# Attention with two-expert routing on one core: the order of the convolutions, of the maxima, of the high parts and of the scatters

## The chip, the cores and the metric

The kernel runs on one core of one Trainium2 chip. The metric is the device time of one launch in microseconds (us). Three runs of the kernel before took 3302.37, 3303.25 and 3305.23 us; the median is 3303.25 us.

## What is computed

The input x is 8 images of 128 channels and 32x32 positions. Each image is normalised over its channels and gets a position table; then

```python
q = conv2d(inp, wq)                 # 1x1
k = conv2d(inp, wk, 1, 1)           # 3x3
v = conv2d(inp, wv, 1, 1)           # 3x3
q = q * cos + rotate_every_two(q) * sin
k = k * cos + rotate_every_two(k) * sin
attn = softmax(q @ k.T * SCALE)     # 8 heads, 1024 x 1024 each
attn = einsum('bhij,hg->bgij', attn, mix)
out  = conv2d(attn @ v, wo) + bo    # then a * sigmoid(g), added to x
```

A second layer follows: each of the 8192 tokens is normalised, sent to its best two of eight experts (128 to 512 to 128, with gelu), and the weighted sum is added. Everything is fp32.

## The kernel before, in words

**Precision.** A fp32 number is split into a high part (fp32r) and a low part (the rest). A product takes three matmuls: high weight with low data, low with high, high with high (`split3`, L662).

**Batches and units.** The attention handles one image (a batch) after the other. A batch has a first stretch ("conv stage" here) and then 16 units of 512 queries: unit u is head u//2, half u%2. The keys of a unit are cut in eight chunks of 128 (`kc`). Batches 1 to 6 are one hardware loop; batches 0 and 7 are written out. In batch b, the units also carry the routing of image b-1 (the first layer's result), and late units prepare the input of image b+1.

**Conv stage.** `conv(b, g)` (L705) makes 12 groups of 128 channels x 512 positions: g 0 to 3 are q, 4 and 5 the lower half of k's channels (heads 0 to 3), 6 and 7 the upper half (heads 4 to 7), 8 to 11 are v. k and v have nine taps of three matmuls each. The four PSUM banks of `conv_bank` (L85) are used in turn by g % 4. Groups 0 to 7 are rotated: VectorE multiplies by cosine and shuffles neighbours (L1311), GpSimd multiplies by sine and adds (L541), ScalarE rounds the high part (`rot_hi`, L1048), VectorE subtracts it (`rot_lo`, L1320). The four scratch halves `rot_a`, `rot_s` (L180) lie in the tile E32. SyncE's queue copies q and k of each head from `src` into the stacks `kst`, `qst` (`stacks`, L377), six DMAs a head; for head 0 it waits for the sixth `rot_lo`. v goes through `v_copy` (L1061), transposes on TensorE (`v_transpose`, L756), `v_hi` (L1067) and `v_lo` (L1345). Between these lie the output projection, gate and routing rows of image b-1, and the maxima and first scores of units 0 and 1.

**Maxima.** Softmax needs a shift for each query. For each of a unit's four blocks of 128 queries TensorE computes scores into a two-bank tile, MA or MB (`max_scores`, L765), VectorE takes the maximum (`take_max`, L1352), ScalarE sums the exponentials (`sums`, L1078), and VectorE works out the shift in 14 tiny instructions (`shifts`, L1357, parts 0, 1 and 2). `max_row` (L776) turns the shifts into two rows of `qst` by way of MA and `row_copy` (L1073). This runs two to three units ahead.

**A unit.** At step kc TensorE runs the six value matmuls of the chunk (`values`, L791, into the two PV banks), one `scores` matmul (L784) six chunks ahead into ST[kc % 2], and, for a coming unit, `max_scores` at steps 1, 3, 5 and 7 (L806 to L851). ScalarE turns each score tile into E32 (`exps`, L1084), GpSimd rounds it into the high part Eh (`cast`, L524), VectorE subtracts into El (`exp_lo`, L1394), and `values` uses both. At the end ScalarE empties the two PV banks, scaled by mix (`evict`, L1090, at step 7), and GpSimd adds them to `acc` from unit 3 on (`add`, L534, at steps 0 and 3). The order on each engine is written by hand, in the functions `unit` and `batch` of GpSimd (L567, L587), TensorE (L806, L853), ScalarE (L1118, L1147) and VectorE (L1519, L1553). An engine runs its instructions in that order; a wait holds all that follow it.

The values of a unit start with a wait for the `evict` of the unit before (L797):

```python
            def values(b, u, kc):
                n = b * UNITS + u
                wait(pe, *low(n, kc))
                for c in range(2):
                    ...
                    if kc == 0:
                        wait(pe, s_ev, 2 * n - 1 + c)
```

and on ScalarE a `sums` stands ahead of that `evict` (L1135, at step 6, where L1121 puts the evictions at step 7).

**Routing.** Units 0 to 5 of a batch carry VectorE's small routing steps (`route`, L1413), units 3 and 4 ScalarE's `row_norm` (L1109). In unit 6 GpSimd copies the rows (`row_pair`, L553), and in units 6 to 9 it issues 16 indirect DMAs, `scatter` (L561), four a unit, at odd steps. The buffer they leave is the one into which SyncE then loads image b+1 (L416 to L421), for `prepare` (L679) from unit 12 on.

Of the kernel before, what the change touches and what calls it, by code (L numbers as in the profile page):

```python
# [6 lines left out]
B, C, IMG = 8, 128, 32  # L7
# [40 lines left out]
def build(nc, x, wq, wk, wv, mix, wo, bo, wr, br, ln_g, ln_b, w1, b1, w2, b2,  # L48
# [18 lines left out]
    with ctx:  # L67
# [17 lines left out]
        def conv_bank(g):  # L85

            return [ST[0][:, :], ST[1][:, :], MB[:, 0:NB], MB[:, NB:2 * NB]][g % 4]

# [91 lines left out]
        rot_a = [E32[:, 2 * i, :] for i in range(2)]  # L180
        rot_s = [E32[:, 2 * i + 1, :] for i in range(2)]
# [172 lines left out]
        def _(sp):  # L354
# [145 lines left out]
        def _(pool):  # L500
# [23 lines left out]
            def cast(b, u, kc):  # L524


                if isinstance(b, int):
                    pool.wait_ge(s_ex, KC * (b * UNITS + u) + kc + 1)
                else:
                    pool.wait_ge(s_ex, ready[kc % 2])  # L530
                    pool.reg_add(ready[1 - kc % 2], ready[kc % 2], 1)
# [9 lines left out]
            def rotate(b, g):  # L541

                a, s = rot_a[g % 2], rot_s[g % 2]
# [23 lines left out]
            def unit(b, u, prev):  # L567
                for kc in range(KC):
                    if prev is not None and u == 6 and kc == 0:
                        paired(prev)  # L570
                    if prev is not None and u == 6 and kc == 1:
                        placed(prev)
# [23 lines left out]
            pool.reg_mov(ready[0], KC * UNITS + 1)  # L596
# [61 lines left out]
        def _(pe):  # L658
# [46 lines left out]
            def conv(b, g, taps=None):  # L705
# [4 lines left out]
                if g >= 4 and (taps is None or taps[0] == 0):  # L710
                    wait(pe, s_rf, b * 8 + g - 3)
                o = conv_bank(g).rearrange("p (y x) -> p y x", x=IMG)
# [93 lines left out]
            def unit(b, u, prev, more):  # L806

                n = b * UNITS + u
                for kc in range(KC):
# [35 lines left out]
                    if kc == KC - 1:  # L845
                        if u < UNITS - 3:
                            if prev is not None and u == 4:
                                pe.wait_ge(s_pr, prev + 2)
                            if more and u == UNITS - 4:
                                pe.wait_ge(s_cent, (b + 1) * 2 + 2)  # L850
# [937 lines left out]
```

## Time and profile before

| | us |
|---|---|
| median of three runs | 3303.25 |
| the profiled execution | 3300.94 |
| its span, first to last instruction | 3299.2 |
| TensorE busy | 2969.2 |
| VectorE busy | 2327.6 |
| ScalarE busy | 1730.2 |
| GpSimd busy | 1530.1 |

The attention (batches 0 to 7) fills the span up to about 2900 us, the experts the rest. In batch 3, which is used as the example, the conv stage starts at 1096.8 us, unit 1 at 1208.1 us, and the next batch's conv stage at about 1459 us. A matmul's duration in the rows is its own latency: in an undisturbed stream the starts lie 0.23 us apart though each lasts 0.39 us. "g" or "idle before" is the time in which an engine had nothing running before an instruction, and the name behind it what ended that.

### The profile page before, as it was taken

The page shows a single profiled execution, that of the slowest core. Times are in us where ns is not written, and L with a number is a line of the kernel's source. Part 1 is how long each engine was busy: PE and PEld are TensorE (multiplying, and loading weights), DVE is VectorE, ACT ScalarE, POOL GpSimd, SP SyncE. Part 2 cuts the span into 40 slices and gives each one's busy share as a digit, 9 for nine tenths or more (in the row PEclk, how much of TensorE's full clock was granted, in tenths as well). Part 3 has the DMA queues.
Part 4 walks back from the last instruction along what each step waited for, and adds up shares of the span by engine and source line. Part 5 has one row for each costly group of instructions (what it writes and reads, how often), then busy time and mean ns, then how long its engine had stood idle before and what let it go on. Part 6 is the DMA issues. An engine that isn't in the chain of part 4 may idle for free.

```text
span 3299.2 us, 45985 instructions
## 1 busy us (share of the span) xinstructions
PE 2969.2 (90%) x13024; PEld 2350.6 (71%) x13024; DVE 2327.6 (71%) x4556; ACT 1730.2 (52%) x2996; POOL 1530.1 (46%) x1729
## 2 busy tenths in 40 slices
PE   7999989898989899898989899898989898949997
PEld 5777777676767777676767677676767677737776
DVE  4688658874888568864978478865887488845664
ACT  2566346542666256643655266634655366626671
POOL 3244515642364425552464335551565236525783
PEclk9999999999999999998999999999999999969998
DMA  4254010101011001101110101101010101216665
GB/s 144 81 210 156 17 26 22 35 15 32 20 31 28 20 24 34 35 2 33 30 33 17 34 20 27 32 18 26 22 33 15 32 20 41 63 59 218 237 227 210
DMA packets 71320, 196.22 MB, mean 59 GB/s; under 512 B 16134, under 2 KB 16720, under 8 KB 71028
## 3 DMA queue, kind: packets, MB, share of 16 engines
q1 hardware_dynamic: 61940, 175.88, 17.4%
q0 software_dynamic: 9088, 16.94, 1.6%
q8 instruction: 123, 2.02, 0.3%
q14 instruction: 169, 1.38, 0.1%
HBM read 39.91 MB, written 63.34 MB: 31 GB/s over the span
## 4 chain that ended last, share of the span: by engine, by line
PE 54%; issue 14%; DVE 10%; POOL 9%; ACT 8%; DMA 3%; SPq 2%; ACTq 0%; POOLq 0%; DVEq 0%
PE PVT L660 34%; PE ST L660 9%; PE MB L660 6%; PE MA L660 5%; DVE nmax L1355 3%; POOL Eh L532 3%; POOL E L545 2%; POOL E L547 2%; ACT tmp L1025 2%; ACT E L1025 2%; POOL rows L563 1%; DMA wt<-wall 1%; DVE El L1397 1%; ACT MA L1025 1%; POOL acc L539 1%
## 5 line engine op out<-in xcount | busy, mean ns | idle before, releaser
L532 POOL CAST Eh<-E 128x512 fp32r<-128x512 f32 x1024 | 684.8, 671 | 1335.1 <-ACT E L1025 1327.0
L1397 DVE TENSOR_TENSOR El<-E,Eh 128x512 fp32r<-128x512 f32 x1024 | 925.6, 905 | 368.1 <-POOL Eh L532 365.1
L660 PE MATMUL PVT<-El,vh 128*128 128x512 f32 x2048 | 849.1, 415 | 158.6 <-ACT tmp L1025 111.0
L1025 ACT ACTIVATE E<-ST 128x512 f32<-128x512 f32 x1024 | 610.4, 598 | 671.9 <-PE ST L660 644.5
L660 PE MATMUL PVT<-Eh,vl 128*128 128x512 f32 x2048 | 819.1, 400 | 0.0
L660 PE MATMUL PVT<-Eh,vh 128*128 128x512 f32 x2048 | 817.2, 399 | 0.0
L660 PEld LDWEIGHTS PVT<-El,vh 128*128 128x128 f32 x2048 | 395.8, 193 | 299.9 <-ACT tmp L1025 125.4
L1025 ACT ACTIVATE MA<-MA,nmax 128x1024 f32<-128x1024 f32 x288 | 313.0, 1087 | 277.7 <-DVE nmax L1355 222.0
L660 PEld LDWEIGHTS PVT<-Eh,vh 128*128 128x128 f32 x2048 | 394.5, 193 | 88.0
L660 PEld LDWEIGHTS PVT<-Eh,vl 128*128 128x128 f32 x2048 | 397.3, 194 | 78.2 <-issue 3.4
L1355 DVE TENSOR_REDUCE nmax<-MA 128x1 f32<-128x1024 f32 x288 | 350.7, 1218 | 96.4 <-PE MA L660 95.6
L660 PE MATMUL ST<-qst,kst 98*128 98x512 f32 x1024 | 412.2, 404 | 0.0
L539 POOL TENSOR_TENSOR acc<-acc,tmp 128x512 f32<-128x512 f32 x224 | 288.3, 1288 | 40.3 <-ACT tmp L1025 40.3
L1355 DVE TENSOR_REDUCE nmax<-MB 128x1 f32<-128x1024 f32 x224 | 273.0, 1219 | 0.3 <-PE MB L660 0.3
L1025 ACT ACTIVATE MB<-MB,nmax 128x1024 f32<-128x1024 f32 x224 | 239.2, 1068 | 17.5 <-DVE nmax L1355 17.4
L660 PE MATMUL MA<-kst,qst 96*128 96x512 f32 x576 | 186.5, 405 | 53.8 <-DMA qst<-src 27.9
L660 PEld LDWEIGHTS ST<-qst,kst 98*128 98x128 f32 x1024 | 196.7, 192 | 44.2 <-ACT E L1025 1.7
L628 POOL DMA_INDIRECT yrows<-xr,idx x156 | 190.9, 1224 | 75.0 <-issue 41.8
L545 POOL TENSOR_TENSOR E<-E,sin_sb 128x512 f32<-128x512 f32 x64 | 90.1, 1408 | 200.4 <-DVE E L1318 200.4
L1025 ACT ACTIVATE src<-E 128x512 fp32r<-128x512 f32 x64 | 40.4, 631 | 268.8 <-POOL E L547 268.8
L1025 ACT ACTIVATE tmp<-PVT,mix_col 128x512 f32<-128x512 f32 x224 | 143.8, 686 | 53.8 <-PE PVT L660 53.7
L1686 DVE TENSOR_TENSOR hl<-h,hh 128x1024 fp32r<-128x1024 f32 x78 | 95.7, 1226 | 103.2 <-ACT hh L1025 85.8
(273 smaller groups left out, 4330.0 us busy)
## 6 DMA issues: line engine op xcount, KB each, us to landing
rows<-xr SPq DMA_DIRECT2D x68, 520.0 KB, 5.6
kst<-src SPq DMA_DIRECT2D x192, 128.0 KB
qst<-src SPq DMA_DIRECT2D x192, 128.0 KB
wt<-wall SPq DMA_DIRECT2D x39, 514.0 KB
wt<-wall SPq DMA_DIRECT2D x39, 512.5 KB
xrow<-rows SPq DMA_DIRECT2D x39, 260.0 KB
wall<-yrows SPq DMA_DIRECT2D x32, 256.0 KB, 4.8
xr<-in_x_dram SPq DMA_DIRECT2D x8, 512.0 KB, 3.5
```

The lines of the kernel that those rows point to most:

```text
L532: nc.gpsimd.tensor_copy(Eh[:, kc, :], E32[:, kc % 4, :]).then_inc(s_eh, 1)
L539: nc.gpsimd.tensor_tensor(acc[:, c, cols], acc[:, c, cols], tmp[:, c, :], ALU.add).then_inc(s_acc, 1)
L545: nc.gpsimd.tensor_tensor(s, s, sin_sb[:, g % 2 * NB:(g % 2 + 1) * NB], ALU.mult).then_inc(s_rot, 1)
L547: nc.gpsimd.tensor_tensor(a, a, s, ALU.add).then_inc(s_rr, 1)
L563: nc.gpsimd.indirect_dma_start(out=rows_d[:, :], out_offset=bass.IndirectOffsetOnAxis(ap=slot[:, i:i + 1], axis=0), in_=xr[c][:, g, :], in ...
L628: nc.gpsimd.indirect_dma_start(out=yrows_d[:, :], out_offset=bass.IndirectOffsetOnAxis(ap=idx[j % XR][:, i:i + 1], axis=0), in_=yrow[j % Y ...
L660: return nc.tensor.matmul(o, w, m, start=start, stop=stop)
L1025: return nc.scalar.activation(o, i, func, **kw)
L1355: nc.vector.tensor_reduce(nmax[:, par, i:i + 1], M[:, :], AX, ALU.max, negate=True).then_inc(s_red, 1)
L1397: tt(El[:, kc, :], E32[:, kc % 4, :], f(Eh[:, kc, :]), ALU.subtract).then_inc(s_lo, 1)
L1686: tt(low, exact, f(high), ALU.subtract).then_inc(t_hl, 1)
```

## The change

1. **Order of the convolutions.** The upper half of k (groups 6 and 7) is convolved after v (groups 8 to 11). `turn` gives the place of each group in that order, from which its bank and its semaphore counts follow. Groups 6 and 7 are rotated in the tiles `tmp` and `eg` instead of E32. The stacks of head 4 wait for the last two `rot_lo`. The order of everything else in the conv stage is rewritten around it, and VectorE rotates group 4 ahead of the first gate.
2. **Maxima at chunks 1, 3, 4 and 6.** TensorE's `max_scores` of steps 5 and 7 move to steps 4 and 6, VectorE's `take_max` with them, ScalarE's `sums` of step 6 to step 5, VectorE's `shifts` parts 1 and 2 from step 6 to step 7.
3. **High parts.** For chunks 1 and 7 ScalarE writes Eh itself, with a second exponential of the same score tile, and GpSimd's cast is gone.
4. **Scatters.** Three a unit at steps 5, 6 and 7 of units 6 to 11 (3, 3, 3, 3, 3, 1) instead of four a unit in units 6 to 9. GpSimd's `add` moves from steps 0 and 3 to steps 1 and 3, `placed` from step 1 to step 4 of unit 6.

```diff
+        turn = [0, 1, 2, 3, 4, 5, 10, 11, 6, 7, 8, 9]
...
-        rot_a = [E32[:, 2 * i, :] for i in range(2)]
-        rot_s = [E32[:, 2 * i + 1, :] for i in range(2)]
+        rot_a = [E32[:, 2 * (g % 2), :] for g in range(6)] + [tmp[:, 0, :], eg[:, 0, :]]
+        rot_s = [E32[:, 2 * (g % 2) + 1, :] for g in range(6)] + [tmp[:, 1, :], eg[:, 1, :]]
...
-                if h == 0:
-                    sp.wait_ge(s_rlo, b * 8 + 6)
+                if h % 4 == 0:
+                    wait(sp, s_rlo, b * 8 + 6 + h // 2)
...
             def cast(b, u, kc):
+                if kc in (1, 7):
+                    return
...
-                    if kc in (0, 3) and u >= 3:
-                        add(b, u - 1, kc // 3)
+                    if kc in (1, 3) and u >= 3:
+                        add(b, u - 1, kc // 2)
...
-                    if prev is not None and 6 <= u < 10 and kc % 2 == 1:
-                        scatter(prev, 4 * u - 24 + kc // 2)
+                    if prev is not None and 6 <= u < 12 and kc in (5, 6, 7) and 3 * u - 23 + kc < 2 * KC:
+                        scatter(prev, 3 * u - 23 + kc)
...
             def batch(b, prev=None):
-                for g in range(8):
+                for g in range(6):
                     rotate(b, g)
-                for kc in range(AHEAD):
+                cast(b, 0, 0)
+                rotate(b, 6)
+                cast(b, 0, 2)
+                rotate(b, 7)
+                for kc in range(3, AHEAD):
                     cast(b, 0, kc)
```

TensorE, in `unit` and then in `batch`:

```diff
+                    if kc == 4 and u < UNITS - 3:
+                        max_scores(b, u + 3, 0, MA, 4 * n + 11)
                     if kc == 5:
-                        if u < UNITS - 3:
-                            max_scores(b, u + 3, 0, MA, 4 * n + 11)
...
-                    if kc == KC - 1:
-                        if u < UNITS - 3:
...
-                            max_scores(b, u + 3, 1, MB, 4 * n + 12)
+                    if kc == 6 and u < UNITS - 3:
...
+                        max_scores(b, u + 3, 1, MB, 4 * n + 12)
...
-                conv(b, 6)
-                conv(b, 7, range(0, 5))
+                conv(b, 8)
+                conv(b, 9)
                 if prev is not None:
                     pe.wait_ge(s_gate, prev * 2 + 2)
                 max_scores(b, 0, 0, MA, 4 * n)
-                conv(b, 7, range(5, TAPS))
                 if prev is not None:
                     route_rows(prev)
+                conv(b, 10, range(0, 5))
                 max_scores(b, 0, 1, MA, 4 * n + 1)
...
+                conv(b, 10, range(5, TAPS))
                 if prev is not None:
                     route_logits(prev)
...
+                max_scores(b, 0, 2, MA, 4 * n + 2)
+                conv(b, 11, range(0, 5))
                 if prev is not None:
                     pe.wait_ge(s_lg, prev + 1)
                 v_transpose(b, 0)
+                max_scores(b, 0, 3, MA, 4 * n + 3)
+                conv(b, 11, range(5, TAPS))
+                max_scores(b, 1, 0, MA, 4 * n + 4)
+                v_transpose(b, 1)
+                conv(b, 6, range(0, 5))
                 max_row(b, 0, 4 * n + 5)
-                conv(b, 10, range(0, 5))
+                conv(b, 6, range(5, TAPS))
                 pe.wait_ge(s_mrow, n + 1)
                 max_scores(b, 1, 1, MA, 4 * n + 5)
-                pe.wait_ge(s_vt, b * 4 + 2)
+                pe.wait_ge(s_vt, b * 4 + 4)
                 scores(b, 0, 0)
+                v_transpose(b, 2)
+                conv(b, 7, range(0, 3))
                 scores(b, 0, 1)
...
                 max_scores(b, 1, 2, MA, 4 * n + 6)
+                conv(b, 7, range(3, 6))
+                v_transpose(b, 3)
                 scores(b, 0, 2)
...
                 max_scores(b, 1, 3, MA, 4 * n + 7)
+                conv(b, 7, range(6, TAPS))
                 scores(b, 0, 3)
...
                 scores(b, 0, 4)
                 max_scores(b, 2, 0, MA, 4 * n + 8)
...
                 scores(b, 0, 5)
+                pe.wait_ge(s_rf, b * 8 + 8)
                 max_scores(b, 2, 1, MB, 4 * n + 8)
```

ScalarE, in `exps`, `unit` and `batch`, and VectorE, in `exp_lo`, `unit` and `batch`:

```diff
+                if kc in (1, 7):
+                    copy(Eh[:, kc, :], ST[1][:, :], ACT.Exp)
                 copy(E32[:, kc % 4, :], ST[kc % 2][:, :], ACT.Exp).then_inc(s_ex, 1)
...
-                    if kc == 6 and u < UNITS - 3:
+                    if kc == 5 and u < UNITS - 3:
                         sums(b, u + 3, 0, MA)
...
-                rot_hi(b, 6)
-                sums(b, 0, 0, MA)
-                rot_hi(b, 7)
+                v_copy(b, 0)
+                v_copy(b, 1)
                 if prev is not None:
                     row_transposed(prev)
+                sums(b, 0, 0, MA)
                 sums(b, 0, 1, MA)
+                v_copy(b, 2)
                 sums(b, 0, 2, MA)
...
                 sums(b, 1, 2, MA)
+                rot_hi(b, 6)
+                v_hi(b, 3)
                 exps(b, 0, 2)
                 sums(b, 1, 3, MA)
                 exps(b, 0, 3)
...
+                rot_hi(b, 7)
                 exps(b, 0, 4)
                 sums(b, 2, 0, MA)
...
-                dve.wait_ge(s_eh, KC * n + kc + 1)
+                if kc in (1, 7):
+                    dve.wait_ge(s_ex, KC * n + kc + 1)
+                else:
+                    wait(dve, s_eh, 6 * n + max(kc, 1))
...
-                    if u < UNITS - 2 and kc == 6:
+                    if u < UNITS - 2 and kc == 7:
                         shifts(b, u + 2, 1)
...
-                    if u < UNITS - 2 and kc == 6:
+                    if u < UNITS - 2 and kc == 7:
                         shifts(b, u + 2, 2)
...
-                    if u < UNITS - 3 and kc in (5, 7):
-                        take_max(b, u + 3, kc // 2 - 2, MA if kc == 5 else MB)
+                    if u < UNITS - 3 and kc in (4, 6):
+                        take_max(b, u + 3, kc // 2 - 2, MA if kc == 4 else MB)
...
+                rotate(b, 4)
+                rot_lo(b, 4)
                 if prev is not None:
                     gate(prev, 0)
-                rotate(b, 4)
-                rot_lo(b, 4)
```

## Rows read from the trace of the kernel before

**Rows 1.** The page: busy us, share of the span and instructions of each engine.

```profile
PE 2969.2 (90%) x13024; PEld 2350.6 (71%) x13024; DVE 2327.6 (71%) x4556; ACT 1730.2 (52%) x2996; POOL 1530.1 (46%) x1729
```

**Rows 2.** Stretches of batch 3: from:to, length, busy us per engine, granted clock, DMA.

```profile
1096.80:1191.30 94.50, 80.15 (x326) 61.73 (x324) 45.05 (x88) 28.66 (x48) 28.52 (x24) 0.91 0.11 29
1208.14:1396.08 187.94, 172.60 (x758) 136.88 (x758) 160.36 (x331) 121.05 (x219) 102.01 (x123) 0.98 0.14 35
1208.14:1223.80 15.66, 15.31 (x69) 12.17 (x69) 13.44 (x37) 10.62 (x20) 5.16 (x8) 1.00 0.23 51
1255.76:1272.35 16.59, 16.29 (x77) 13.12 (x77) 14.79 (x33) 12.22 (x25) 8.24 (x10) 1.00 0.00 1
1325.32:1344.30 18.98, 15.29 (x68) 12.16 (x68) 15.68 (x28) 10.87 (x20) 12.55 (x14) 1.00 0.05 16
1396.08:1413.88 17.80, 17.34 (x72) 12.78 (x73) 15.22 (x29) 10.57 (x20) 7.59 (x10) 1.00 0.00 1
```

**Rows 3.** Waits of TensorE over the span: us in total, times, longest us.

```profile
PE PVT L660 <- ACT tmp L1025: 111.0, 85, 3.7
PE PVT L660 <- DVE vl L1349: 37.5, 15, 3.0
...
PE MA L660 <- DMA qst<-src: 27.9, 7, 6.1
PE MA L660 <- ACT MA L1025: 24.4, 8, 3.8
```

**Rows 4.** Timeline of TensorE and ScalarE where unit 1 ends: start, us, instruction.

```profile
1222.82 0.62 PE L660 MATMUL MB<-kst,qst 96*128 96x512 f32 x2
1223.80 0.50 PE L660 MATMUL PVT<-El,vh 128*128 128x512 f32 x1 [0.35 <-ACT acc L1025]
...
1221.96 1.09 ACT L1025 ACTIVATE MA<-MA,nmax 128x1024 f32<-128x1024 f32 x1
...
1223.06 1.26 ACT L1025 ACTIVATE acc<-PVT,mix_col 128x512 f32<-128x512 f32 x2
```

**Rows 5.** Timeline of unit 8, a unit with scatters: GpSimd, VectorE, ScalarE, TensorE.

```profile
1329.27 1.30 POOL L539 TENSOR_TENSOR acc<-acc,tmp 128x512 f32<-128x512 f32 x1
...
1329.34 2.32 DVE L1397 TENSOR_TENSOR El<-E,Eh 128x512 fp32r<-128x512 f32 x1 [1.52 <-POOL Eh L532]
...
1339.32 1.25 POOL L563 DMA_INDIRECT rows<-xr,slot  x1 [0.17 <-ACT E L1025]
...
1341.14 1.21 DVE L1355 TENSOR_REDUCE nmax<-MA 128x1 f32<-128x1024 f32 x1
...
1342.47 1.09 ACT L1025 ACTIVATE MA<-MA,nmax 128x1024 f32<-128x1024 f32 x1 [3.29 <-DVE lman L1376]
...
1343.35 0.69 DVE L1397 TENSOR_TENSOR El<-E,Eh 128x512 fp32r<-128x512 f32 x1
...
1344.30 0.50 PE L660 MATMUL PVT<-El,vh 128*128 128x512 f32 x1 [3.70 <-ACT tmp L1025]
```

**Rows 6.** Groups over the span: count | busy us, mean ns | idle before.

```profile
L532 POOL CAST Eh<-E 128x512 fp32r<-128x512 f32 x1024 | 684.8, 671 | 1335.1 <-ACT E L1025 1327.0 <-issue 3.9 <-POOL xr L554 1.2
L1025 ACT ACTIVATE E<-ST 128x512 f32<-128x512 f32 x1024 | 610.4, 598 | 671.9 <-PE ST L660 644.5 <-DVE El L1397 26.7 <-issue 0.2
...
```

**Rows 7.** Timeline, batch 3 conv stage: TensorE stall, two conv matmuls, VectorE's sixth `rot_lo`.

```profile
1136.33 0.73 PE L660 MATMUL MA<-kst,qst 96*128 96x512 f32 x2 [3.62 <-DMA qst<-src]
...
1145.60 0.40 PE L660 MATMUL ST<-xl,wch 128*128 128x512 f32 x1
1145.84 0.40 PE L660 MATMUL ST<-xh,wcl 128*128 128x512 f32 x1
...
1129.81 0.69 DVE L1324 TENSOR_TENSOR src<-E,src 128x512 fp32r<-128x512 f32 x1 [3.43 <-ACT src L1025]
```

**Rows 8.** Next image: DMA issue (page; last: us to landing), its first matmul.

```profile
xr<-in_x_dram SPq DMA_DIRECT2D x8, 512.0 KB, 3.5
...
1400.54 1.12 PE L660 MATMUL MB<-xr,mean_w 128*128 128x512 f32 x2 [0.17 <-ACT MB L1025]
```

More of the change, by code:

```diff
@@ L529, in cast @@
                 else:
-                    pool.wait_ge(s_ex, ready[kc % 2])
-                    pool.reg_add(ready[1 - kc % 2], ready[kc % 2], 1)
+                    pool.wait_ge(s_ex, ready[i])
+                    pool.reg_add(ready[1 - i], ready[i], 2 if kc in (0, 6) else 1)
                 nc.gpsimd.tensor_copy(Eh[:, kc, :], E32[:, kc % 4, :]).then_inc(s_eh, 1)
@@ L570, in unit @@
                         paired(prev)
-                    if prev is not None and u == 6 and kc == 1:
+                    if prev is not None and u == 6 and kc == 4:
                         placed(prev)
@@ L595, in _ @@
             batch(0)
-            pool.reg_mov(ready[0], KC * UNITS + 1)
+            pool.reg_mov(ready[1], KC * UNITS + 1)
             with pool.Fori(1, B - 1) as b:
@@ L709, in conv @@
                     pe.wait_ge(s_xin, b + 1)
-                if g >= 4 and (taps is None or taps[0] == 0):
-                    wait(pe, s_rf, b * 8 + g - 3)
-                o = conv_bank(g).rearrange("p (y x) -> p y x", x=IMG)
+                if taps is None or taps[0] == 0:
+                    if 4 <= turn[g] < 10:
+                        wait(pe, s_rf, b * 8 + turn[g] - 3)
+                    elif turn[g] >= 10:
+                        wait(pe, s_vt, b * 4 + turn[g] - 9)
+                o = conv_bank(turn[g]).rearrange("p (y x) -> p y x", x=IMG)
                 every = [4] if kind == 0 else list(range(TAPS))
@@ L844, in unit @@
                             prefix(prev)
-                    if kc == KC - 1:
-                        if u < UNITS - 3:
[L847 to L850, printed above, removed]
-                            max_scores(b, u + 3, 1, MB, 4 * n + 12)
+                    if kc == 6 and u < UNITS - 3:
+                        if prev is not None and u == 4:
+                            pe.wait_ge(s_pr, prev + 2)
+                        if more and u == UNITS - 4:
+                            pe.wait_ge(s_cent, (b + 1) * 2 + 2)
+                        max_scores(b, u + 3, 1, MB, 4 * n + 12)
             def batch(b, prev=None, more=True):
@@ L1050, in rot_hi @@
                 act.wait_ge(s_rr, b * 8 + g + 1)
-                copy(src[:, 2 * kind, c, hf * NB:(hf + 1) * NB].bitcast(f32r), rot_a[g % 2]).then_inc(s_rhi, 1)
+                copy(src[:, 2 * kind, c, hf * NB:(hf + 1) * NB].bitcast(f32r), rot_a[g]).then_inc(s_rhi, 1)
             def out_hi(n, hf):
@@ L1061, in v_copy @@
             def v_copy(b, g):
[L1062 removed]
+                act.wait_ge(s_cv, b * 12 + 6 + g + 1)
                 if g >= 2:
                     wait(act, s_vT, b * 4 + g - 1)
[L1065 removed]
+                copy(vt[g % 2][:, :], conv_bank(turn[8 + g])).then_inc(s_vt, 1)
             def v_hi(b, g):
@@ L1182, in batch @@
                 exps(b, 0, 3)
-                v_copy(b, 3)
-                v_hi(b, 2)
+                rot_hi(b, 7)
                 exps(b, 0, 4)
                 sums(b, 2, 0, MA)
-                v_hi(b, 3)
                 exps(b, 0, 5)
@@ L1585, in batch @@
                     shifts(b, 0, part)
+                v_lo(b, 0)
                 take_max(b, 1, 0, MA)
-                v_lo(b, 0)
+                v_lo(b, 1)
+                rotate(b, 6)
                 take_max(b, 1, 1, MA)
                 exp_lo(b, 0, 0)
-                v_lo(b, 1)
+                v_lo(b, 2)
+                exp_lo(b, 0, 1)
                 take_max(b, 1, 2, MA)
-                exp_lo(b, 0, 1)
+                rot_lo(b, 6)
+                v_lo(b, 3)
                 exp_lo(b, 0, 2)
                 take_max(b, 1, 3, MA)
-                exp_lo(b, 0, 3)
+                rotate(b, 7)
                 for part in range(3):
                     shifts(b, 1, part)
-                v_lo(b, 2)
+                exp_lo(b, 0, 3)
                 take_max(b, 2, 0, MA)
                 exp_lo(b, 0, 4)
-                v_lo(b, 3)
+                rot_lo(b, 7)
                 take_max(b, 2, 1, MB)
```

45 lines of the change are left out of this document (13 added, 32 removed).

## Prediction

> **What bounds the kernel now.** I read the page first: TensorE is busy for 2969.2 of 3299.2 us, every other engine far less [rows 1]. So only two things can shorten the kernel: TensorE's pauses, and the stretches at half clock. Next the stretches of batch 3. A plain unit lasts 15.66 us with 15.31 busy, so it has almost no pause; unit 8, with scatters, lasts 18.98 us with the same 15.29 busy; units 1 to 11 together last 187.94 us; the conv stage has 80.15 busy in 94.50 us at a mean granted clock of 0.91, that is partly at 1.2 instead of 2.4 GHz [rows 2]. The table of waits then names the pauses: 111.0 us in 85 waits for an eviction of the PV banks, at the start of a unit, 37.5 us for `v_lo`, 27.9 us for head 0's stacks, 24.4 us for a `sums` [rows 3].
>
> The timeline shows why the eviction is late. When unit 1 ends, ScalarE starts the `sums` of unit 4's first block at 1221.96, which holds it till 1223.06; only then come the two evictions (1.26 us), though the first bank was complete about 1 us earlier. TensorE issued its last two matmuls at 1222.82; at 0.23 us each it could have gone on at 1223.28 and starts at 1223.80, 0.52 us late [rows 4]. In a unit with scatters the same queue is longer: the maximum on VectorE starts at 1341.14, the `sums` only at 1342.47 after 3.29 us of idleness, and TensorE starts 3.70 us late at 1344.30 [rows 5]. The maximum was ready long before, but VectorE's order puts it behind an El subtraction and six shift instructions, and that subtraction waits for a cast which stands behind an add and a scatter on GpSimd.
>
> **The change, part by part.**
>
> *Maxima at steps 4 and 6.* Nothing is added. The first block's `sums` leaves step 6, next to the eviction, for step 5. Counting with T as the start of chunk 7's values: the first bank is done at T + 0.9, ScalarE is then free (its chunk-4 exponential ends about T + 0.35), so the first eviction ends at T + 1.6 and TensorE can go on at T + 1.7, against T + 1.6 at which it is ready. Of the 0.52 us some 0.1 stays: 0.4 us a plain unit, 15.66 to 15.25. The reuse of MA and MB costs nothing: `sums` of the same tile ends 1.8 us before the earlier `max_scores` in a plain unit. What is late next is the shift. The last maximum is issued at T - 0.46 and starts on VectorE at T + 0.2; a maximum and part 1 of the shifts behind it take 2.2 us (1341.14 to 1343.35 [rows 5]), then come an El subtraction and part 2 with some 0.9 together: T + 3.3, and TensorE reaches `max_row` at T + 3.4. It just fits, with no cover left. In units from 3 on an add holds VectorE once more: a subtraction that should take 0.69 takes 2.32 us beside a 1.30 us add [rows 5]. I put such units at 15.5.
>
> *Two high parts on ScalarE.* GpSimd loses 256 casts of 0.67 us, ScalarE gains 256 exponentials of 0.60 us (153 us) against 671.9 us of idleness ahead of its exponentials [rows 6]. They fall in steps 1 and 3, which have no `sums`. ScalarE is then at 12 of 15.3 us in a plain unit, nearly full in units 3 and 4 with `row_norm`. The bounds: nothing, or 0.60 on the path in each of 128 units (77 us). I take nothing, since a score tile is used again only two steps, 3.5 us, later.
> The trace shows the subtraction stretched beside the add, as said [rows 5]. The Trainium skill (SBUF — State Buffer, "SBUF: two separate sides") says that a VectorE instruction with two SBUF inputs and a GpSimd instruction that reads SBUF exclude each other for their whole length, and that ScalarE never waits. By that rule the two missing casts free VectorE too, by at most 2 x 0.67 us a unit; my sum has nothing for it.
>
> *Scatters.* 16 indirect DMAs as before, 1.25 us each [rows 5], three in a row at steps 5 to 7, each behind a cast. With six casts (4.0), two adds (2.6) and three scatters (3.8) GpSimd has 10.4 us a unit, where it had 12.55 in unit 8 [rows 2]. Chunks 4 to 6 get their high part up to 1.3 us later, chunk 6 is needed last of all, and no eviction stands behind them any more. So I put units 7 to 10 at 15.7, unit 6 with its row copy at 16.0, unit 11 at 15.5. Unit 4 has 0.9 us more matmuls (it is 16.59 with 16.29 busy [rows 2]): 16.4. With two plain units at 15.25 and units 3, 5, 11 at 15.5 the sum is 30.5 + 46.5 + 16.4 + 16.0 + 62.8 = 172.2 against 187.94: **-15.7 us a batch**. Unit 12 starts 0.4 us sooner (17.80 to 17.4 [rows 2]).
> The last scatter moves from unit 9 to unit 11, step 5, and SyncE's queue holds the load of the next image behind it. That scatter starts about 13.1 us into the unit, lands some 2.5 us later (an estimate from its 1.25), the load takes 3.5 us and its issue 0.5: 19.6 us. The image's first matmul comes 4.46 us into unit 12 (1400.54 - 1396.08 [rows 2, 8]), so at 19.8. Nothing to one microsecond a batch; I take nothing.
>
> *Conv stage.* The matmuls are the same. Head 0's stacks still wait for the sixth `rot_lo` (1129.81), because the rotation of group 4 is now ahead of the gate and that of group 5 behind it: same time. But TensorE now has two whole groups of v (54 matmuls, starting every 0.24 us [rows 7], 13.0 us) before it needs them, where it had 14 taps (42 matmuls, 10.1 us): the 3.62 us stall [rows 7] falls to 0.7. The two `v_lo` stalls at the first values, 37.5 us in 15 waits [rows 3] and so 2.5 us each, vanish, since v is ready before. New waits stand in for them: `v_copy` of the third group waits for the first v transpose and holds a `sums` (2.0 us); VectorE's queue with rotation 6, and ScalarE's with `rot_hi` 6 and 7, hold the maxima of unit 1 (0.5 + 3.7 + 2.3) and chunk 4's exponential and `sums` inside unit 0 (1.2 + 2.4). Laid out by hand, unit 0's second half of values (1191.3 now [rows 2]) starts at 1183.6, and 3.6 us are lost again behind it: -4, with a microsecond for the clock **-5 us a batch**. The bounds are far apart: -10 (the new waits hidden) to +4 (each twice as long).
>
> **Sum.** Six looped batches: -(15.7 + 0.4 + 5) = -21.1, together -127. Batch 7, which prepares no image, -19. Batch 0 has no scatters: 13 units of -0.4 and -4 in the conv stage, -9. That is -155. I keep 12 us back, 1.5 a batch, for waits of the new order that a hand schedule overlooks: **-143**. The profiled execution, 3300.94 us (span 3299.2), goes to 3158; it lies 2.3 us below the median of 3303.25, which goes to **3160 us**.
>
> **Rivals.**
> *A, the shift becomes the bound.* VectorE's chain to `max_row` has no slack, and VectorE is busy for 15.7 us in unit 8 [rows 2]. For it: the 2.32 us subtraction. Against: the adds fall at other steps. If `max_row` waits 0.5 to 0.6 us in each of 12 units a batch, 52 us go: about 3210.
> *B, the scatters in a row cost as much as before.* A cast behind each scatter is late by 1.25 us, three times. Against: nothing that ends a unit waits for them. If units 6 to 10 keep 1.6 us each, 56 us go in seven batches: 3216. The Trainium skill (SBUF — State Buffer, the box on SWDGE) says that a VectorE operation on the shared port keeps GpSimd from writing descriptors; by that rule it is three scatters in a row that would suffer.
> *C, everything moved is hidden.* The conv stage gives 10 us a batch and VectorE's freed time takes the rest: 3303 - 185 = 3118.
> *D, slower.* One mechanism: `max_row` held by the shifts, by so much that the unit is longer than now. Units 1 to 11 average 17.1 us now [rows 2]. With -40 us from the conv stages the change loses once they last over some 17.6 us, which means part 2 ending at T + 5.6, 2.3 us later than I count; the last maximum and the subtraction would each have to meet an add. At 17.9 us in every unit it is +0.8 x 11 x 7 and, for batch 0's 13 plain units, +2.2 each: 3303 + 62 + 29 - 40 = 3354.
> *E, nothing.* Should the pause at a unit's start move whole to another step, the time stays 3300.
>
> **How the numbers follow.** Forecast 0.68; A 0.14; B 0.05; C 0.08; D 0.03; E 0.02. The forecast's own range is 3130 to 3190. The middles of A, B and C lie inside 3115 to 3225, but each has a spread of some 30 us either way (the conv stage's bounds alone are -5 and +9 us in eight batches, -40 and +72), so this range holds about 8 in 10. What a measurement can tell from no change is about 0.2%, 6.6 us. All but D and E are faster by more: faster 0.95, same 0.02, slower 0.03.
>
> **What would show it.** Right: waits for the eviction fall from 111 us to under 30, plain units last 15.2 to 15.4 and units 7 to 10 under 16.2, El waits on GpSimd less, the `v_lo` stall is gone and the stack stall is below 1.5 us. New small waits before `max_row`'s MA matmuls and for `sums` late in the conv stage. Wrong: a wait for VectorE's `mc` of over 0.3 us in each unit (A, D), units 7 to 10 above 17 (B), a wait for the image's DMA in unit 12, or a longer conv stage.

## The result, and the profile after

The changed kernel takes **3246.37 us** (median of 4 runs, 3242.84 to 3250.75), the kernel before 3303.01 beside it: ratio 0.9828, 95% interval 0.9811 to 0.9845. That is 56.6 us less where 143 were forecast, and outside both ranges (3130 to 3190, and the wider 3115 to 3225). Its profiled execution took 3247.52 us.

The page of the changed kernel, busy time by engine, against [rows 1]:

```profile
PE 2948.0 (91%) x13024; PEld 2298.3 (71%) x13024; DVE 2381.6 (73%) x4556; ACT 1877.4 (58%) x3252; POOL 1362.3 (42%) x1473
```

TensorE is busy for 21.2 us less with the same 13,024 matmuls. It ran longer at the full clock: the mean granted clock of the profiled span is 0.965, and was 0.949. ScalarE has the 256 new exponentials, GpSimd lost 256 casts. Next TensorE's waits, as in [rows 3]:

```profile
PE MA L670 <- ACT MA L1039: 79.1, 43, 3.8
PE MA L670 <- DVE mc L1408: 78.0, 109, 2.6
...
PE MA L670 <- DMA qst<-src: 11.3, 10, 3.1
```

The 111.0 us for evictions and the 37.5 us for `v_lo` are gone, the wait for the stacks fell from 27.9 to 11.3. In their place stand 78.0 us for `mc`, the input of `max_row`, in nearly every unit, and three times the wait for a `sums` in bank MA (24.4 before). The stretches of batch 3: units 1 to 11, the plain unit 1, unit 4, unit 6 (the row copy), unit 8, unit 12:

```profile
1195.63:1376.85 181.22, 171.28 (x758) 132.67 (x757) 162.72 (x330) 133.83 (x241) 87.16 (x101) 1.00 0.14 33
1195.63:1211.62 15.99, 15.47 (x69) 11.93 (x68) 13.72 (x37) 11.77 (x22) 4.13 (x6) 1.00 0.22 49
1243.53:1261.61 18.08, 16.54 (x79) 12.94 (x78) 16.03 (x34) 13.61 (x27) 6.56 (x8) 1.00 0.00 0
1277.51:1295.53 18.02, 15.39 (x70) 12.02 (x69) 16.25 (x27) 11.88 (x22) 9.38 (x12) 1.00 0.02 5
1311.97:1327.86 15.89, 15.38 (x69) 12.02 (x69) 13.93 (x25) 11.89 (x22) 9.67 (x12) 1.00 0.04 14
1376.85:1394.99 18.14, 17.63 (x73) 12.55 (x72) 15.78 (x29) 11.98 (x22) 6.76 (x8) 1.00 0.10 31
```

Against [rows 2]: units 1 to 11 last 181.22 us instead of 187.94, and 172.2 was the forecast. Unit 8 went from 18.98 to 15.89, as forecast. The plain unit, forecast at 15.25, went *up* from 15.66 to 15.99, unit 4 from 16.59 to 18.08, unit 12, forecast at 17.4, from 17.80 to 18.14. `max_row` waits in each of the eleven: 0.52, 0.52, 0.55, 1.54, 0.34, 2.63, 0.88, 0.51, 1.01, 0.51, 0.94 us, together 9.95 of idle time, a little more than the 9.0 that are missing.

How the wait comes about is seen where unit 1 gives way to unit 2 (the chunk 7 of unit 1 starts at T = 1209.98). Timeline of VectorE, then GpSimd's cast and TensorE:

```profile
1210.18 1.23 DVE L1371 TENSOR_REDUCE nmax<-MB 128x1 f32<-128x1024 f32 x1
1211.33 0.15 DVE L1392 SCALAR_TENSOR_TENSOR lman<-lman,lfit 128x4 f32<-128x4 f32 x1
...
1212.31 0.16 DVE L1402 TENSOR_TENSOR shft<-shft,lfit 128x4 f32<-128x4 f32 x1
1212.40 0.18 DVE L1460 SCALAR_TENSOR_TENSOR ny<-nt,ny 128x16 f32<-128x16 f32 x1
1212.52 0.69 DVE L1416 TENSOR_TENSOR El<-E,Eh 128x512 fp32r<-128x512 f32 x1
1213.13 0.58 DVE L1406 CAST mc<-shft 128x4 fp32r<-128x4 f32 x1
1213.74 0.16 DVE L1408 TENSOR_TENSOR mc<-shft,mc 128x4 fp32r<-128x4 f32 x1
...
1212.89 0.80 POOL L538 CAST Eh<-E 128x512 fp32r<-128x512 f32 x1 [1.81 <-ACT E L1039]
...
1214.04 0.40 PE L670 MATMUL MA<-identr,mc 128*2 128x128 f32 x4 [0.52 <-DVE mc L1408]
```

The maximum starts at T + 0.20, as worked out ahead, and the subtraction at T + 2.54, 0.1 later. But the small cast into `mc`, 128x4, takes 0.58 us where it takes 0.17 with nothing beside it: it ends as GpSimd's cast of a high part does (1212.89 + 0.80 = 1213.69). So `mc` is ready at T + 3.92 instead of T + 3.3. TensorE's last matmul before it started at 1213.12, so it could have gone on at 1213.36 or so, T + 3.4 as forecast, and goes on at T + 4.06: 0.7 us late. The 0.52 in the row is less because it counts from the end of that matmul, whose own latency runs on.

A wait can cost more than its length. The 2.63 us of unit 6 are the same in batches 3 and 4, but the unit lasts 18.02 us in one and 19.6 in the other. The stretch of unit 6 in batch 4, to be set beside the fourth line above:

```profile
1630.31:1649.92 19.61, 16.98 (x69) 13.16 (x69) 16.25 (x27) 11.97 (x22) 9.38 (x12) 0.91 0.01 5
```

The mean granted clock is 0.91 there and 1.00 in batch 3: after the pause TensorE ran for a while at the lower of its two levels (1.2 instead of 2.4 GHz).

### The profile page after: what moved, and what is told of

Same layout as the page of the kernel before. It is cut to its first block and busy times, and to the rows that moved or that the text cites. A ratio compares the mean times of both kernels' runs of the same rounds, so it can differ in the third digit from the quotient of the medians.

```text
span 3245.8 us, 45775 instructions
## 1 busy us (share of the span) xinstructions
PE 2948.0 (91%) x13024; PEld 2298.3 (71%) x13024; DVE 2381.6 (73%) x4556; ACT 1877.4 (58%) x3252; POOL 1362.3 (42%) x1473
## 5 line engine op out<-in xcount | busy, mean ns | idle before, releaser
L538 POOL CAST Eh<-E 128x512 fp32r<-128x512 f32 x768 | 536.9, 700 | 1499.9 <-ACT E L1039 1499.0
L1416 DVE TENSOR_TENSOR El<-E,Eh 128x512 fp32r<-128x512 f32 x1024 | 950.9, 931 | 225.9 <-POOL Eh L538 222.6
L670 PE MATMUL PVT<-El,vh 128*128 128x512 f32 x2048 | 836.3, 408 | 0.0
L670 PE MATMUL PVT<-Eh,vl 128*128 128x512 f32 x2048 | 809.7, 395 | 0.0
L670 PE MATMUL PVT<-Eh,vh 128*128 128x512 f32 x2048 | 808.6, 395 | 0.0
L545 POOL TENSOR_TENSOR acc<-acc,tmp 128x512 f32<-128x512 f32 x224 | 295.2, 1321 | 44.9 <-ACT tmp L1039 44.9
L670 PE MATMUL MA<-kst,qst 96*128 96x512 f32 x576 | 195.1, 421 | 60.0 <-ACT MA L1039 48.2
L670 PEld LDWEIGHTS ST<-qst,kst 98*128 98x128 f32 x1024 | 195.9, 191 | 58.0 <-ACT E L1039 15.4
L1039 ACT ACTIVATE tmp<-PVT,mix_col 128x512 f32<-128x512 f32 x224 | 153.7, 688 | 98.5 <-PE PVT L670 98.2
L670 PEld LDWEIGHTS MA<-kst,qst 96*128 96x128 f32 x576 | 106.1, 197 | 110.7 <-ACT MA L1039 58.0
L1039 ACT ACTIVATE Eh<-ST 128x512 fp32r<-128x512 f32 x256 | 153.1, 598 | 34.3 <-PE ST L670 34.2
```

The source lines that it names most:

```text
L538: nc.gpsimd.tensor_copy(Eh[:, kc, :], E32[:, kc % 4, :]).then_inc(s_eh, 1)
L545: nc.gpsimd.tensor_tensor(acc[:, c, cols], acc[:, c, cols], tmp[:, c, :], ALU.add).then_inc(s_acc, 1)
L670: return nc.tensor.matmul(o, w, m, start=start, stop=stop)
L1039: return nc.scalar.activation(o, i, func, **kw)
L1416: tt(El[:, kc, :], E32[:, kc % 4, :], f(Eh[:, kc, :]), ALU.subtract).then_inc(s_lo, 1)
```

## The experiments

The change has four parts here: 1 the order of the convolution, 2 the maxima with the shifts' parts 1 and 2 from step 6 to step 7, 3 the high parts, 4 the scatters and adds. Ratios are to the kernel before, measured beside each.

**e1, the shifts back at step 6.** On VectorE only, all four parts kept otherwise:

```diff
-                    if u < UNITS - 2 and kc == 7:
+                    if u < UNITS - 2 and kc == 6:
                         shifts(b, u + 2, 1)
...
-                    if u < UNITS - 2 and kc == 7:
+                    if u < UNITS - 2 and kc == 6:
                         shifts(b, u + 2, 2)
```

> The changed kernel with one part undone: VectorE makes parts 1 and 2 of the shifts at step 6 again, ahead of the last maximum, not at step 7. Theory V: the gain that is missing went into TensorE's wait for the shifts (mc) at max_row, 78.0 us in 109 waits, because parts 1 and 2 stand behind the last maximum on VectorE. Then this wait falls below 15 us, no other wait at the unit's start takes its place, plain units last 15.2 to 15.4 us instead of 15.8 to 16.0, and the time is 3150 to 3185 us. Rival P: VectorE is held by GpSimd's casts and adds wherever the shifts stand (they met casts at step 7); then max_row waits half as long as now and the time is 3195 to 3225. Rival N: the eviction wait returns or ScalarE's two extra exponentials set the pace; time 3235 to 3255.

**3183.77 us** (3181.66 to 3185.22), ratio 0.9651 [0.9630, 0.9672]: 62.6 us below the change. Its waits of TensorE, then its stretches (units 1 to 11, unit 1, unit 4):

```profile
PE MA L670 <- ACT MA L1039: 79.8, 46, 3.6
...
PE MA L670 <- DVE mc L1408: 8.7, 21, 0.6
```

```profile
1170.90:1345.31 174.41, 170.72 (x759) 133.24 (x758) 165.88 (x326) 134.00 (x241) 88.73 (x101) 1.00 0.14 34
1170.90:1186.18 15.28, 15.28 (x69) 12.01 (x68) 13.73 (x38) 11.75 (x22) 4.10 (x6) 1.00 0.23 51
1216.95:1234.28 17.33, 16.85 (x77) 12.93 (x77) 17.02 (x37) 13.46 (x27) 6.32 (x9) 1.00 0.00 0
```

The plain unit has no pause left: 15.28 long, 15.28 busy. The `mc` waits fell by 69.3 us, and the time by nearly that. The place of eight small instructions a unit (parts 1 and 2) cost 62.6 of the 119 us that the kernel gives with them at step 6.

**e2, part 2 alone** on the kernel before (shifts at step 7, as in the change).

> The kernel before with part 2 of the change alone (maxima at steps 4 and 6, sums at step 5, shifts parts 1 and 2 at step 7); casts, scatters and convolutions as before. Theory V: the eviction waits (111 us) go, and a wait for mc at max_row comes in every unit, somewhat longer than in the changed kernel since GpSimd has all casts: 90 to 130 us. Time 3260 to 3295. Rival: the maxima alone are the whole gain, 3240 to 3255, and the other parts give nothing.

3305.92 us, ratio 1.0014 [1.0, 1.0027]: nothing gained, where I had expected 3260 to 3295. The size of the `mc` waits was as expected; that they would eat the whole gain was not.

```profile
PE MA L660 <- DVE mc L1391: 97.2, 108, 4.0
PE PVT L660 <- DVE vl L1348: 37.1, 15, 3.0
...
PE PVT L660 <- ACT tmp L1024: 6.0, 7, 0.9
```

The wait for evictions went from 111.0 to 6.0 us, and 97.2 us for `mc` came in its place: one wait swapped for another.

**e7, part 2 alone with the shifts at step 6.**

> The kernel before with the order of the maxima of the change on all engines, but the shifts left at step 6, where they were; no other part of the change. With the shifts at step 7 the same edit measured 3305.92 us, nothing gained. Theory V (only the place of the shifts gave the gain away): TensorE's waits for the eviction fall from 111 us below 40 us and no mc waits of the size of the 97 us come in their place; 3215 to 3245 us. Rival (the gain needs the high parts or the scatters of the change too, or VectorE has no time left in a unit): mc or eviction waits stay above 80 us together, 3270 us or more.

3228.56 us, ratio 0.9794 [0.9775, 0.9814]: `mc` waits 31.3 us in 26, eviction waits 8.2. Against e2 the place of the shifts alone is worth 0.022, that is 73 us of 3300. Left are the units with scatters: units 6 to 9 of batch 3 last 17.40, 16.27, 16.60 and 18.88 us.

**e3, part 1 alone.**

> The kernel before with part 1 of the change alone (upper half of k convolved last, with the new order of the conv stage on every engine). The comparison of the two traces puts the conv stage, from the last eviction of a batch to the first of the next, at 111 to 113 us before and 108.3 to 109.5 after; so theory: 3 us a batch, 3275 to 3285 us. Rival: the conv stage gives the whole gain of the change (7 us a batch, 3245 to 3255), or in the surroundings of the old units nothing at all (3300 to 3306).

3288.55 us (3275.53 to 3294.82), ratio 0.9964 [0.9948, 0.9980]. The `v_lo` waits go, the waits for a `sums` grow to 83.2 us, and the evictions keep their 112.4: some 12 us in all, a little less than the 18 to 28 expected.

**e5, part 4 undone in the change** (adds at steps 0 and 3, scatters at the odd steps of units 6 to 9).

> The changed kernel with part 4 undone: four scatters a unit at odd steps in units 6 to 9, adds at steps 0 and 3, the row copy's placing at step 1. Theory V says that GpSimd's load matters only through the casts and adds that hold VectorE's shifts; units 7 to 9, now 16.44, 15.89 and 16.6, get longer by 0.5 to 1.5 us, unit 4 (18.1) and unit 6 (18.0 to 19.6), whose adds and row copy stand at step 1 behind a held shift, shorter: 3240 to 3265 us. Rival S: the new scatter places carry a large part of the gain, 3275 to 3295.

3254.35 us, ratio 0.9871 [0.9845, 0.9897] against 0.9828: 8 us slower by the medians, 14 by the ratios, whose intervals just touch, with `mc` waits of 82.0. The time is in V's range, its units are not: unit 4 stays at 18.09 us, and unit 6 or 7 of a looped batch lasts up to 20.5.

**e8, parts 1 and 2 of the shifts together, still at step 7:**

```diff
                     if u < UNITS - 2 and kc == 7:
                         shifts(b, u + 2, 1)
+                        shifts(b, u + 2, 2)
...
-                    if u < UNITS - 2 and kc == 7:
-                        shifts(b, u + 2, 2)
```

> The changed kernel, parts 1 and 2 of the shifts still at step 7, but part 2 directly behind part 1, ahead of the routing operation and the El subtraction. This takes 0.7 to 1.3 us out of the way of mc in each unit and nothing else. Theory V1 (mc is 0.5 us late because of what stands between the parts and the GpSimd cast that it meets there): mc is ready at T+2.9 instead of T+3.9, mc waits fall from 78 us below 20 us, 3185 to 3205 us. Rival V2 (step 7 is late whatever stands between, since part 1 only begins at T+1.3 behind the maximum): mc waits stay above 50 us, above 3225 us.

3223.32 us, ratio 0.9766 [0.9748, 0.9784], `mc` waits 36.0 us in 31: below V2's bounds, above V1's. V1 holds in the first units: 15.40, 15.15 and 15.62 us in batch 3, as with step 6, so what stood between the parts and the cast met there is what made them late. V1 missed that at step 7 the chain now meets GpSimd in a unit with scatters. Batches 1, 2, 6 and 7 have a unit 9 of 20.0 to 21.6 us. VectorE, GpSimd and TensorE in that of batch 2, then the stretch of this unit:

```profile
967.48 0.66 DVE L1402 TENSOR_TENSOR shft<-shft,lfit 128x4 f32<-128x4 f32 x1
968.17 1.87 DVE L1406 CAST mc<-shft 128x4 fp32r<-128x4 f32 x1
...
967.18 0.98 POOL L569 DMA_INDIRECT rows<-xr,slot  x1 [0.17 <-issue]
968.17 0.62 POOL L538 CAST Eh<-E 128x512 fp32r<-128x512 f32 x1
968.75 1.26 POOL L545 TENSOR_TENSOR acc<-acc,tmp 128x512 f32<-128x512 f32 x1
...
970.37 0.37 PE L670 MATMUL MA<-identr,mc 128*2 128x128 f32 x2 [3.70 <-DVE mc L1408]
...
964.79:986.32 21.53, 17.83 (x70) 13.85 (x69) 16.83 (x28) 11.98 (x22) 10.18 (x13) 0.84 0.20 47
```

A cast of four columns takes 1.87 us, as long as GpSimd's cast and add beside it (968.17 to 970.01), and TensorE stands for 3.70 us. The unit loses more than that, since the clock falls to its lower level behind the pause (0.84 over the unit). The rows before the change had already shown a subtraction held by two instructions of GpSimd in a row: the 2.32 us of [rows 5] are not the add alone (it ends at 1330.57), but also the cast behind it, which the subtraction outlasts by 0.55 us.

```profile
1330.50 0.61 POOL L532 CAST Eh<-E 128x512 fp32r<-128x512 f32 x1
```

**e10, the cast tested by itself:** the changed kernel, part 2 by reductions.

```diff
-                    nc.vector.tensor_copy(mc[:, par, :, 0], z).then_inc(s_ch, 1)
+                    one = z.rearrange("p (a o) -> p a o", o=1)
+                    nc.vector.tensor_reduce(mc[:, par, :, 0], one, AX, ALU.max).then_inc(s_ch, 1)
...
-                    tt(mc[:, par, :, 1], z, f(mc[:, par, :, 0]), ALU.subtract).then_inc(s_ch, 1)
+                    nc.vector.tensor_reduce(mc[:, par, :, 1], one, AX, ALU.max, negate=True).then_inc(s_ch, 1)
```

> The changed kernel with the two small instructions of part 2 of the shifts, the cast of z (128x4) and the subtraction z - mc, replaced by two reductions over an axis of length one, at the same place in VectorE's order and with the same waits. Left out: the low part of the row mc (the second column gets the negated z instead), so the output is another one. Theory L (VectorE's cast and its subtraction are held by the GpSimd cast that runs beside them, 0.58 us in a plain unit where 0.17 is usual; an instruction with one SBUF input and no fast mode is not held): the reductions take 0.2 us each even beside a GpSimd cast, mc is ready 0.4 us sooner, mc waits fall from 78 us to 35 to 50 us, 3205 to 3225 us. Rival (the cast is late for a reason of its own, or everything on VectorE waits beside GpSimd): the first reduction has a mean above 0.4 us like the cast (474 ns), mc waits stay within 10 us of 78, 3240 us or more.

The groups of the changed kernel (two lines) and of this one (two lines): count | busy us, mean ns.

```profile
L1406 DVE CAST mc<-shft 128x4 fp32r<-128x4 f32 x128 | 60.7, 474 | 0.7
L1408 DVE TENSOR_TENSOR mc<-shft,mc 128x4 fp32r<-128x4 f32 x128 | 27.2, 213 | 4.4
```

```profile
L1409 DVE TENSOR_REDUCE mc<-shft 128x4 fp32r<-128x4 f32 x128 | 20.2, 158 | 4.4
L1407 DVE TENSOR_REDUCE mc<-shft 128x4 fp32r<-128x4 f32 x128 | 19.2, 150 | 0.7
```

And the place that was shown above, VectorE, GpSimd, TensorE:

```profile
1211.81 0.15 DVE L1407 TENSOR_REDUCE mc<-shft 128x4 fp32r<-128x4 f32 x1
1211.99 0.16 DVE L1409 TENSOR_REDUCE mc<-shft 128x4 fp32r<-128x4 f32 x1
...
1211.55 0.82 POOL L538 CAST Eh<-E 128x512 fp32r<-128x512 f32 x1 [1.81 <-ACT E L1039]
...
1212.28 0.34 PE L670 MATMUL MA<-identr,mc 128*2 128x128 f32 x3
```

Both run at once, inside GpSimd's cast, and TensorE no longer waits. Over the whole trace, 190 of these reductions have a cast of GpSimd beside them and the longest takes 0.16 us; of the casts into `mc` in the changed kernel 97 have one, with a median of 0.58, and the 16 with nothing beside them have 0.17. So theory L holds for the instructions. For the time it is less clear: `mc` waits 47.9 us and a plain unit lasts 15.4 to 15.6, but that is the fastest run (3214.57); the runs go up to 3243.01, the median is 3233.48 us, 8 above the range, and the ratio, 0.9809 [0.9791, 0.9826], overlaps that of the change. Batch 4 of the profiled run has a unit 9 of 21.31 us where the others have 16.5 to 16.7: there the El subtraction ahead of the reductions is held for 2.49 us (1659.83), and the reductions take 0.14 and 0.16 us behind it. Whether this makes the runs differ by 28 us was not tried.

**Parts 3 and 4.** e4 is the change without part 3; e6 is e1 without part 3, e11 e1 without part 4, e12 e1 without both.

> The changed kernel with all eight high parts cast by GpSimd again, the shifts still at step 7. Beside shifts at step 6 the two casts cost nothing (3182.42 against 3183.77 us). Theory P (where VectorE's chain to mc is the bound, each instruction held by a GpSimd cast shows; chunk 7's cast of the unit lies beside part 1 or 2): 10 to 40 us slower than the 3246 us of the changed kernel, mc waits above 90 us. Rival (the casts fall where VectorE does nothing that is due): 3240 to 3252 us, mc waits 70 to 85 us.

> The changed kernel with parts 1 and 2 of the shifts back at step 6 (that kernel measured 3183.77 us) and GpSimd casting all eight high parts again. Left of the change: order of the convolution, order of the maxima, scatters. Theory H (the high parts on ScalarE are cover: GpSimd has room for two more casts in a unit, except where adds and scatters are): 3184 to 3200 us, plain units still 15.2 to 15.5 us, the loss in units 7 to 12. Rival (GpSimd's casts hold VectorE's small operations and scatters everywhere): above 3210 us, with mc waits back above 40 us in the execution.

> The kernel of the first experiment (3183.77 us, shifts at step 6) with the scatters and adds at their old steps. In the changed kernel the same edit cost 8 us. Theory G (once no eviction or shift waits behind them, where the scatters stand matters little): 3184 to 3200 us. Rival B (scatters at two places of a unit, with a cast between, still delay the El subtractions that the values need): 3210 us or more, units 7 to 9 above 17 us.

> The kernel before with the order of the convolution and of the maxima of the change, shifts at step 6, and neither the high parts on ScalarE nor the moved scatters and adds. Measured so far, as ratio to before: maxima alone 0.9794, all but the high parts 0.9651, all but the scatters 0.9663, all 0.9651. Theory S (parts 3 and 4 are two ways to one room on GpSimd: either is enough, and without both units 6 to 9 last 17.4, 16.1, 16.5 and 19 to 20 us as with the maxima alone): ratio 0.973 to 0.977, 3212 to 3226 us, the convolution stages giving 0.003 to 0.006. Rival (the convolution order gives all of the 0.013 to 0.014 that lies between maxima alone and the others): 0.966 or less, 3190 us or less, with units 6 to 9 below 17 us.

| kernel | parts | shifts | us | ratio [95%] |
|---|---|---|---|---|
| change | 1 2 3 4 | 7 | 3246.37 | 0.9828 [0.9811, 0.9845] |
| e4 | 1 2 4 | 7 | 3241.73 | 0.9813 [0.9797, 0.9830] |
| e1 | 1 2 3 4 | 6 | 3183.77 | 0.9651 [0.9630, 0.9672] |
| e6 | 1 2 4 | 6 | 3182.42 | 0.9651 [0.9634, 0.9669] |
| e11 | 1 2 3 | 6 | 3191.89 | 0.9663 [0.9647, 0.9679] |
| e12 | 1 2 | 6 | 3225.88 | 0.9767 [0.9742, 0.9793] |

The high parts give nothing beside the scatters' new steps, in either place of the shifts (theory P fell: `mc` waits 56.8 us in e4, not above 90, and below the rival's 70 too). The scatters give next to nothing beside the high parts: G holds. Without both, 0.010 to 0.012 is lost, some 35 us: S holds in the time. The loss lies where it should, in the units with scatters: units 6, 8 and 10 of batch 4 last 17.41, 16.42 and 16.35 us in e12, and 15.26, 15.24 and 15.53 in e1. That both parts make the same room on GpSimd is my reading of this, not a thing measured by itself. Unit 9 was expected at 19 to 20 us and lasts 16.9 in most batches; the one of batch 3 (20.44 us) is the exception, VectorE, GpSimd, TensorE:

```profile
1313.48 2.21 DVE L1402 CAST mc<-shft 128x4 fp32r<-128x4 f32 x1
...
1312.83 0.99 POOL L566 DMA_INDIRECT rows<-xr,slot  x1 [0.15 <-issue]
1313.83 0.62 POOL L535 CAST Eh<-E 128x512 fp32r<-128x512 f32 x1
1314.41 1.26 POOL L542 TENSOR_TENSOR acc<-acc,tmp 128x512 f32<-128x512 f32 x1
...
1316.02 0.42 PE L668 MATMUL MA<-identr,mc 128*2 128x128 f32 x4 [3.24 <-DVE mc L1404]
```

**e9, a better order in the conv stage, on top of e1.** VectorE's queue, and likewise on ScalarE `sums(b, 0, 2, MA)` ahead of `v_copy(b, 2)` and `exps(b, 0, 4)` ahead of `rot_hi(b, 7)`:

```diff
                 take_max(b, 1, 1, MA)
+                take_max(b, 1, 2, MA)
                 exp_lo(b, 0, 0)
                 v_lo(b, 2)
                 exp_lo(b, 0, 1)
-                take_max(b, 1, 2, MA)
                 rot_lo(b, 6)
+                take_max(b, 1, 3, MA)
                 v_lo(b, 3)
                 exp_lo(b, 0, 2)
-                take_max(b, 1, 3, MA)
                 rotate(b, 7)
+                take_max(b, 2, 0, MA)
                 for part in range(3):
                     shifts(b, 1, part)
                 exp_lo(b, 0, 3)
-                take_max(b, 2, 0, MA)
```

> The kernel of the first experiment (3183.77 us) with another order in the convolution stage alone: ScalarE takes the sums of chunk 2 of unit 0 ahead of the third copy of v, and the fifth exponential ahead of the last high part of k; VectorE takes the maxima of chunks 2 and 3 of unit 1 and chunk 0 of unit 2 as soon as TensorE has given them, ahead of the El and v_lo subtractions and of the shifts of unit 1. Theory Q (the 79.8 us of waits for ScalarE's sums are a place in VectorE's and ScalarE's queue: the gaps of 1.8, 3.5, 1.6 and 3.6 us in batch 3): they fall to half or less, the conv stage is 5 to 8 us shorter in each of seven batches, 3130 to 3150 us. Rival (the chain of maximum, sums and next scores through the one bank MA is itself the bound, about 3.5 us a link): at most 3 us a batch, 3165 us or more.

**3109.53 us** (3107.63 to 3118.87), ratio 0.9423 [0.9407, 0.9439], the fastest of all, below even Q's range. One of TensorE's two long waits for a `sums` in batch 3 of e1 (timeline; the other, in unit 0, is 3.56 us), then the table of waits of e9 and the longest that is left there:

```profile
1142.16 0.75 PE L670 MATMUL MA<-kst,qst 96*128 96x512 f32 x1 [3.49 <-ACT MA L1039]
```

```profile
PE MA L670 <- DVE mc L1408: 31.6, 30, 3.3
...
PE MA L670 <- ACT MA L1039: 15.6, 24, 1.2
```

```profile
1122.06 0.48 PE L670 MATMUL MA<-identr,mc 128*2 128x128 f32 x4 [2.99 <-DVE mc L1408]
```

79.8 us of waits for `sums` became 15.6, while those for `mc` rose from 8.7 to 31.6. The chain through bank MA was not the bound; its maxima stood behind subtractions that are needed only later. Between the profiled executions of e1 and e9 (62.8 us) TensorE's idle time falls by 51.4 us and its busy time by 11.4, with a mean granted clock of 0.971 against 0.967. Which of the moved instructions gave it was not separated. Next in line is `max_row` of unit 1, 2.99 us.

## Why the prediction was wrong, by its own steps

From the first eviction of batch 1 to that of batch 6, a batch takes (mean of the five, profiled executions) 363.12 us before, 354.45 after, 345.58 in e1 and 338.18 in e9. The forecast was -21.1 a batch; the change gave -8.7, e1 -17.5.

*The step that failed* is the one on the shifts: "then come an El subtraction and part 2 with some 0.9 together: T + 3.3 ... It just fits, with no cover left." Maximum and part 1 came when I said. A routing instruction that I had not counted took 0.12 us ahead of the subtraction, and part 2 took 0.77 us instead of some 0.3, since its cast waited out a cast of GpSimd. `mc` came at T + 3.92 where TensorE was there at T + 3.4. With its start at T + 4.06 that is 0.7 us on the path of a plain unit (15.99 against 15.28 in e1), with idle time of 0.52, and of up to 2.63 where more meets: 78.0 us of idle time. It is the sign of being wrong that the prediction named, a wait for `mc` of over 0.3 us in each unit. A sum that ends in "no cover left" should have had the wait as its likeliest case.

In the prediction I weighed the Trainium skill (SBUF — State Buffer, "SBUF: two separate sides") only for the El subtractions and, in rival B, for the scatters. The section says that the lock on the shared port is taken also by a VectorE instruction in a fast mode, and its box on SWDGE names an fp32 copy from SBUF to SBUF as one; under "Who interferes with whom" it says that a reduction never contends. By that rule the cast into `mc` waits and a reduction does not. The trace agrees: 0.58, 1.87 and 2.21 us beside GpSimd's work, 0.15 us for the reduction inside it (e10). The information was there for the one instruction with no slack.

*Rival A* was what happened, in mechanism and nearly in the plain units' size (0.5 to 0.6 us forecast, 0.52 idle and 0.7 on the path measured). With 52 us it was priced too low: the place of the shifts cost 62.6, since units 4 (1.54) and 6 (2.63) wait longer. Rival D asked for units of 17.6 us on average, and they last 16.5 (181.22 / 11). Of B nothing shows: units 7 to 10 last 15.9 to 16.6 us, and the issues of the scatters, which by the rule named there would suffer, have a mean of 1.03 us after against 1.21 before.

*Maxima at steps 4 and 6*: right. Eviction waits 111.0 to 6.0 (e2), and 15.28 us in e1 against 15.25.

*High parts*: costless in the sum, as said (e6 against e1, e4 against the change), though not in each unit. With them unit 4 of batch 3 lasts 17.33 us and unit 12 18.54 (e1), without them 16.83 and 17.68 (e6); unit 13 goes the other way, 16.91 against 20.60 in batch 4. What makes it so was not tried. *Scatters*: unit 8 right (15.7 against 15.89). That either part alone does the work of both I had not seen.

*Unit 4*: 17.33 us in e1 against 16.4. TensorE is busy for 16.85 of them, where [rows 2] had 16.29, and 0.5 are pauses. The maxima's new steps alone bring most of it: in batch 3 it lasts 17.30 in e7, which has only these, and 16.57 in e3, which lacks them. How was not tried. This term is 0.9 short a batch. *Unit 12* was forecast at 17.4 and lasts 18.14 after and 18.54 in e1, 0.7 to 1.1 short; that too was not followed up.

*Conv stage*: from the last eviction of a batch to the next one's first (mean over the five from batch 1 to 6) 111.9 us before, 109.35 after, 108.9 in e1: -2.6 to -3.0 against -5. The new waits had been read from the queues nearly right in sum, 12.1 us against 11.3 in batch 3, but not each: one wait of 3.50 where 3.7 and 2.3 stood, and 3.57 for the 2.4. The way in which the term was to come about did not hold. I had counted 4 us fewer pauses and one for the clock; TensorE's idle time in these stretches is 14.5 us before, 15.9 after and 15.9 in e1, and what fell is the time at the lower clock, 21.8, 13.7 and 12.3 us. Half of the 8.1 us less at the lower level is 4.0, and less the 1.4 of idle time that is the 2.6 measured: what the change gained here came from the clock, not from fewer pauses. e9 took out the 3.50 and has 2.99 us for `mc` in place of the 3.57: 8.5 us of idle time, 100.2 us in all.

*Sum*: with the shifts in their place e1 gives -119 of the forecast's -143, inside the range. So one term, 63 us, made the miss. The working without the 12 us kept back said -21.1 a batch and e1 has -17.5: the conv stage is some 2 short, units 1 to 11 about 1 (mostly unit 4), and the units from 12 on the rest. The 12 us kept back covered a part of that.

## What to carry to other kernels

When a wait is moved off one engine, write down the slack of the next chain in the same units as its instructions, and count with their stretched durations: where the slack is smaller than one instruction of GpSimd, expect that chain to be the new bound. Place a chain of tiny dependent instructions by who waits for it, and test its place alone, as it costs a line or two. In a queue written by hand, put what frees a bank or starts another engine ahead of work that only has to be done some time.

## What the runs showed of the hardware

A 128x4 cast on VectorE (0.17 us alone) took 0.58 us beside a cast of GpSimd. Where a cast and an add of GpSimd follow each other without a gap, it took 1.87 us, the time of both together (e8), and 2.21 where it began 0.35 us earlier, beside the end of a scatter's issue (e12): VectorE did not come in between the two. A small subtraction beside a scatter's issue took 0.66 (e8). A reduction with the same source and destination took 0.15 us beside the same cast. In these rows the cost of a VectorE instruction goes by its kind and by what it meets, not by its size.

Pauses of TensorE of 2.6 to 3.7 us were followed in some places, not in all, by a stretch at the lower clock level: in e8 the values matmuls behind the 3.70 us pause start 0.43 us apart instead of 0.23.
